# Input loads, weight splits and constants reordered at the start of an attention and mixture-of-experts layer, two vector steps moved in its ending

## The chip, the cores and the metric

The kernel runs on one core of one Trainium2 chip. The metric is the device time of one execution in microseconds. A measurement is the median of several runs; the profile comes from one further execution with its own time.

## What is computed

`x` has the shape 8 x 750 x 256, everything in fp32. Three stages follow each other for each of the 8 batch entries:

```
# 1. tokens: three shifted copies side by side, one linear layer
x = concatenate([input[:, o:o + 744, :] for o in (0, 3, 6)], axis=-1)
h = einsum('btd,od->bto', x, W) + b                       # 8 x 744 x 256
# 2. causal attention, 16 heads of 16, on the layer norm of h
h = h + softmax(mask(q k^T / sqrt(16))) v @ Wp.T + bp
# 3. four experts of width 1024, the best two of each token
logits = layernorm(h) @ wr + br
y = gelu(x @ w1[e] + b1[e]) @ w2[e] + b2[e]
c = gelu(b1) @ w2 + b2 ; c_sum = c.sum(axis=0)
out = h + sum_k gates_k * (y_sel - c_sel + c_sum)
```

`c`, `c_sum` and `b2 - c + c_sum` depend on the weights alone. The kernel calls them `crow`, `csum` and `dall`.

## The kernel before, in words

The program is written out by hand in one function, `layer`, with one block for each engine. A list of events sets the order of work, and every engine walks the same list and does its share of each event, with semaphores in between. `front_events` is the list ahead of the first batch entry, `body_events` that of one entry (it also holds the front work of the next one), and `ending` that of the experts' stage. The body runs 8 times; the last entry's rest is done in the ending, beside the first expert tiles.

**Opening.** SP (SyncE) issues twelve loads at lines 530 to 541: the token weights transposed (`tok_stage`, which lies in `prob`), the q, k and v weights, two bias rows, the token weights as they are (`tok_raw`, which lies in `spare`), the router's weights `wr_sb` (256 x 4), bias columns, the router's bias, and the output projection's weights twice (`wp_rows` in `spare`, `projw`). POOL (GpSimd) fills all constants (lines 661 to 687), among them three rows of ones in each of the four stacks `kst` (line 674), which are 3 partitions of 2976 elements. PE (TensorE) waits at the head of its block for all those constants and for five of the loads (`extra_loaded`). Then it multiplies the token weights by the router's weights, 12 products (line 1302), the projection's weights likewise, 4 products (line 1306), and the bias columns and `ones`, 6 products (line 1311). The results are extra router columns that ride along with the token product and the projection: `DA` is 256 + 4. These products are fp32, and the trace counts two records for each. DVE (VectorE) copies the results out (lines 964 to 968), and only then does ACT (ScalarE) round `tok_stage` with its new columns and `qkv_stage` into fp32r (lines 823, 824). DVE subtracts for the low halves (lines 971, 972). Every fp32 product later is made of three: high by high, high by low, low by high.

ACT loads `x` for the first entry (line 854) after both splits (`w_split` 2). POOL splits it into high and low (lines 700, 703), twice, once for each half of the 256 features. Then PE does the token product, 6 tiles of 18 matmuls (line 1329), and DVE adds the bias and takes the statistics (lines 987 to 995). POOL takes the root (line 708), DVE normalises (line 1001), PE turns the tiles (line 1349).

**q and k.** Eight `qk` events follow. For each PE multiplies, ACT, DVE and POOL cut the result into three bf16 parts (lines 902, 1015, 751, 753) in one of three buffers `parts`, and SP stores it to DRAM (line 548). `load_stack` n reads the parts back from DRAM as the stack of four heads, six DMAs for each n (line 562). It waits until the stores of its half are done. The first `mx` events (products of q and k whose row maxima DVE takes, lines 1389, 1031 and 1028) need stack 0 alone.

```
    for m in range(KC):
        for n in range(4):
            yield "qk", 4 * m + n
        yield "load_stack", 2 * m
        yield "load_stack", 2 * m + 1
```

**Ending.** `const` 0 and 1 are the products for `crow` (PE line 1462, 96 records in all; DVE line 1253). At the end of `const` 1, DVE also forms `csum` and `dall` in 8 instructions (lines 1256 to 1263). Two `flip` events turn the first tile of rows (PE 1446, ACT 950, DVE 1238), and the expert tiles start: `l1` is a first-layer product (PE 1481, gelu on ACT 935, high and low on DVE 1269 and 1271), `l2` a second-layer product (PE 1497), `y` the scaling of a finished tile on DVE (1283). `l2` number n waits for the low half of `l1` number n, and the first `l2` of a tile waits for `y` of the tile before. ACT reads `dall` at `offs` (line 945), first after `l1` 8. The last entry's projection, norm, gates, count, places, the expert table and the scatters are put beside the steps by the dictionary `BESIDE`. The table (DVE lines 1197 to 1232, 17 instructions) tells which rows the tiles from number 4 on take.

## Time and profile before

| | |
|---|---|
| median of 3 runs | 1761.87 us |
| the runs | 1755.54, 1761.87, 1763.46 us |
| the profiled execution, its own time | 1770.43 us |
| its span, from the first to the last instruction | 1768.7 us |
| busy: PE, weight loads (PEld), DVE, ACT, POOL | 86%, 67%, 62%, 40%, 47% |
| mean granted TensorE clock | 0.936 |

The profiled execution took 8.6 us more than the median. 1.7 us of its time lie outside its span. A busy share is an average over stages with different limits; the opening has hardly any PE work in it, and the ending almost nothing else. All times below are microseconds from the start of the span.

### The profile page before, as it was taken

The numbers are of one execution on the slowest core, as the hardware profiler recorded it, in microseconds if no ns is written. First come the engines' busy times: TensorE is split into PE (matmuls) and PEld (weight loads), VectorE is DVE, ScalarE is ACT, GpSimd is POOL, SyncE is SP. The second block draws the span as 40 slices with busy tenths as digits, with TensorE's granted clock in tenths as the row PEclk, the third lists the DMA queues.
The fourth block names the chain that finished last, engine by engine and source line by source line (L and its number), as shares of the span: only waits on it lengthen the run. The fifth ranks groups of instructions, "written<-read, shape, count | busy, mean of one in ns | idle before, by whom it ended". The sixth has DMA issues, their size and how long they took to land.

```text
span 1768.7 us, 33228 instructions
## 1 busy us (share of the span) xinstructions
PE 1522.5 (86%) x10648; PEld 1184.5 (67%) x10648; DVE 1100.8 (62%) x3476; ACT 707.0 (40%) x1463; POOL 837.1 (47%) x912
## 2 busy tenths in 40 slices
PE   2659898798898897898987877889999999999997
PEld 2626565474474474464654432789999999999997
DVE  1356678678678677778686571555555555555554
ACT  0104554444444544634544445133333333333332
POOL 4313434644644645736546335055455545554545
PEclk9859999898898998999998888899999999999999
DMA  2151543653643644635626675255555564645451
GB/s 89 61 136 49 153 111 102 158 134 103 154 124 106 162 118 130 162 100 163 147 78 165 151 249 177 79 177 173 201 186 186 180 204 157 215 162 188 169 189 46
DMA packets 166972, 256.24 MB, mean 145 GB/s; under 512 B 30484, under 2 KB 97998, under 8 KB 166800
## 3 DMA queue, kind: packets, MB, share of 16 engines
q1 hardware_dynamic: 108816, 166.66, 32.5%
q10 hardware_dynamic: 34368, 50.33, 9.1%
q0 software_dynamic: 23616, 37.12, 7.4%
q8 instruction: 87, 1.43, 0.3%
q14 instruction: 85, 0.70, 0.1%
HBM read 173.92 MB, written 75.29 MB: 141 GB/s over the span
## 4 chain that ended last, share of the span: by engine, by line
PE 53%; DVE 13%; DMA 11%; issue 10%; SPq 5%; ACT 4%; POOL 3%; ACTq 0%; DVEq 0%; POOLq 0%
PE yb L1497 15%; PE l1b L1481 14%; PE pab L1329 6%; PE pvb L1429 6%; PE stb L1406 4%; PE mxb L1389 4%; DMA qk_s<-parts 4%; DMA qst<-negp 4%; DVE unused L1028 4%; SPq L594 2%; DVE mxp L1031 1%; PE rb L1446 1%; SPq L562 1%; SPq L578 1%; ACT hf L935 1%
## 5 line engine op out<-in xcount | busy, mean ns | idle before, releaser
L849 ACT ACTIVATE prob<-stb 124x496 f32<-124x496 f32 (+2 forms) x832 | 397.9, 505 | 412.4 <-PE stb L1406 393.7
L1389 PE MATMUL mxb<-kst,qst 96*124 96x372 bf16 (+4 forms) x1024 | 314.6, 339 | 98.8 <-DVE mxp L1028 57.4
L1028 DVE CUSTOM_DVE_ANT_0 unused<-mxb,mask_row 124x372 bf16<-124x372 f32 (+4 forms) x768 | 351.7, 483 | 70.6 <-PE mxb L1389 67.5
L1497 PE MATMUL yb<-w2p,hp 128*128 x2448 | 334.5, 282 | 15.3 <-DVE yo L1283 15.3
L1406 PE MATMUL stb<-qst,kst 99*124 99x372 bf16 (+4 forms) x1024 | 307.3, 333 | 45.2 <-DMA qst<-negp 21.8
L1481 PE MATMUL l1b<-x2T,w1s 128*128 128x384 f32 x1632 | 338.9, 343 | 1.2 <-DVE x2T L1238 1.2
L1497 PEld LDWEIGHTS yb<-w2p,hp 128*128 128x128 f32 x2448 | 320.1, 189 | 25.9 <-issue 25.8
L935 ACT ACTIVATE hf<-l1b,b1c 128x384 f32<-128x384 f32 x272 | 158.3, 582 | 351.2 <-PE l1b L1481 347.5
L1481 PEld LDWEIGHTS l1b<-x2T,w1s 128*128 128x128 f32 x1632 | 276.6, 190 | 1.6 <-DVE x2T L1238 1.6
L1389 PEld LDWEIGHTS mxb<-kst,qst 96*124 96x124 bf16 x1024 | 138.1, 143 | 190.8 <-DVE mxp L1028 102.1
L1269 DVE CAST hp<-hf 128x384 fp32r<-128x384 f32 x272 | 107.6, 396 | 235.9 <-ACT hf L935 231.0
L1406 PEld LDWEIGHTS stb<-qst,kst 99*124 99x124 bf16 x1024 | 133.7, 140 | 172.7 <-ACT prob L849 85.6
L736 POOL TENSOR_SCALAR_AFFINE_SELECT prob<-prob 124x496 f32<-124x496 f32 x192 | 118.7, 626 | 263.0 <-ACT prob L849 261.6
L1429 PE MATMUL pvb<-prob,vaug 124*17 124x372 f32 (+2 forms) x2304 | 196.0, 458 | 3.5 <-POOL prob L736 3.5
L725 POOL DMA_INDIRECT xs<-xrow,place x96 | 132.4, 1379 | 109.8 <-issue 109.8
L1271 DVE TENSOR_TENSOR hp<-hf,hp 128x384 fp32r<-128x384 f32 x272 | 163.5, 601 | 9.4
L797 POOL DMA_INDIRECT acc<-out,xg x102 | 108.5, 1064 | 121.0 <-DMA out<-acc,xg 97.3
L1031 DVE TENSOR_REDUCE mxp<-mxb 124x1 f32<-124x372 f32 (+1 forms) x256 | 129.8, 507 | 53.2 <-PE mxb L1389 49.1
L803 POOL TENSOR_TENSOR acc<-acc,yo 128x256 f32<-128x256 f32 x102 | 82.3, 823 | 132.4 <-DVE yo L1283 71.9
L1329 PE MATMUL pab<-tokw,xp 128*124 128x260 f32 x864 | 118.5, 293 | 17.7 <-POOL xp L703 17.7
L1329 PEld LDWEIGHTS pab<-tokw,xp 128*124 128x124 f32 x864 | 110.5, 189 | 18.8 <-issue 17.7
L806 POOL DMA_INDIRECT out<-acc,xg x102 | 107.7, 1056 | 26.3 <-issue 20.7
(176 smaller groups left out, 1493.1 us busy)
## 6 DMA issues: line engine op xcount, KB each, us to landing
w1s<-ws SPq DMA_DIRECT2D x34, 2048.0 KB, 9.2
qk_s<-parts SPq DMA_DIRECT2D x64, 279.0 KB, 5.8
xg<-xs SPq DMA_DIRECT2D x34, 396.0 KB, 3.7
kst<-qk_s SPq DMA_DIRECT2D x32, 279.0 KB, 3.8
qst<-qk_s SPq DMA_DIRECT2D x32, 279.0 KB, 5.2
wraw<-in_w_all ACTq DMA_DIRECT2D x32, 256.0 KB, 6.2
ws<-whi ACTq DMA_DIRECT2D x32, 256.0 KB, 2.8
ws<-wlo ACTq DMA_DIRECT2D x32, 256.0 KB, 5.5
```

The lines of the kernel that those rows point to most:

```text
L725: pool.indirect_dma_start(out=xs, out_offset=bass.IndirectOffsetOnAxis(ap=place[:, k, i:i + 1].bitcast(u32), axis=0), in_=xrow[:, i, :], i ...
L849: act.activation(dst, src, ACT.Exp, scale=DH ** -0.5).then_inc(exp_done, 1)
L935: act.activation(hf[:, n % HFB, :], l1b[n % L1B][:, 0:TILE], ACT.Gelu, bias=b1c[:, bass.ds(owners[t] * NM + m, 1)]).then_inc(gelu_done, 1)
L1028: done = dve.tensor_tensor_reduce(out=unused[:, n % 2, e * w:(e + 1) * w], in0=src, in1=mask_row[:, T - w:T], scale=1.0, scalar=-3.0e38, o ...
L1031: done = dve.tensor_reduce(top, src, AX.X, ALU.max)
L1271: dve.tensor_tensor(hp[1][:, n % HPB, :], hf[:, n % HFB, :], hp[0][:, n % HPB, :].bitcast(fp32), ALU.subtract).then_inc(h_split, 1)
L1329: done = nc.tensor.matmul(out, lhs[x][c], rhs[w][c], start=(n == 0), stop=(n == len(steps) - 1))
L1389: done = nc.tensor.matmul(out, qst[g % NG][0:ROWS, h + e, TT * i:TT * i + TT], kst[g % NG][0:ROWS, h + e, k0:k0 + w], start=True, stop=True)
L1406: done = nc.tensor.matmul(out, kst[g][:, h, TT * j:TT * j + TT], qst[g][:, h, q0:q0 + w], start=True, stop=True)
L1429: done = nc.tensor.matmul(pvb[2 * DH * h:2 * DH * h + DH + 1, s, q0 - s * HALF:q1 - s * HALF], vaug[:, j, HG * (g % NG) + h, :], p, start= ...
L1481: done = nc.tensor.matmul(l1b[n % L1B][:, 0:TILE], w1s[t % 2][:, w, c, 128 * m:128 * m + 128], x2T[x][:, t % 2, c, :], start=(k == 0), sto ...
L1497: done = nc.tensor.matmul(yb[i][:, 0:D], hp[x][:, n % HPB, 128 * i:128 * i + 128], w2p[w][:, bass.ds(owners[t], 1), m, :], start=(m == 0 a ...
```

## The change

Five edits, all of order:

1. **Loads.** SP now issues `tok_raw` and `wr_sb` first, then `tok_stage`, bias columns, `wp_rows`, the token bias row, q, k, v, the other bias rows and `projw`. ACT issues the two loads of `x` as its first instructions. There are new semaphores: `raw_loaded` for the first two, `tokw_loaded` for `tok_stage`.
2. **Splits.** The 256 plain columns of the token weights are split without the router's columns, which are split by themselves once they are there. PE starts the 12 router products as soon as `raw_loaded` says so, and waits for the bias columns, `wp_rows` and the router's bias (`extra_loaded`, now 3 loads) only ahead of the other 10. Those 10 go to the second PSUM bank. PE's wait ahead of the token product, `w_split` 2, no longer covers the q, k and v weights.
3. **Constants.** POOL fills `ones`, splits `x`, and only then fills the other constants, the `kst` rows last. The waits for them stand where they are first used.
4. **Stack loads.** In `front_events`, `qk` 4 and 5 come ahead of `load_stack` 0 and 1.
5. **Ending.** The 8 instructions of `csum` and `dall` become an event `sum` behind step 3 of the experts, and the table moves from step 9 to step 10.

```
@@ front_events
-    yield "x_load", 0
-    for p in range(2 * KC):
-        yield "x", p
...
-    for m in range(KC):
-        for n in range(4):
-            yield "qk", 4 * m + n
-        yield "load_stack", 2 * m
-        yield "load_stack", 2 * m + 1
+    for n in range(8):
+        yield "qk", n
+        if n in (5, 7):
+            yield "load_stack", n - 5
+            yield "load_stack", n - 4
@@ ending, BESIDE
             for kind, n in BESIDE.get(at, ()):
                 yield "tail", kind, n
+            if at == 3:
+                yield "expert", "sum", 0
...
-          8: [("place", 0), ("place", 1)], 9: [("table", 0)]}
+          8: [("place", 0), ("place", 1)], 10: [("table", 0)]}
@@ gpsimd
+            pool.memset(ones[:, :], 1.0).then_inc(ones_ready, 1)
+            pool.wait_ge(ones_ready, 1)
...
+            for p in range(2 * KC):
+                emit([("x", p)], 0, 0)
+            pool.memset(vaug[:, :, :, :], 1.0).then_inc(zeroed, 1)
...
+            pool.wait_ge(route_consts, 13)
+            for g in range(NG):
+                if g:
+                    pool.wait_ge(kst_ones, g)
+                pool.memset(kst[g][ROWS:ROWS + NPART, :, :], 1.0).then_inc(kst_ones, 1)
@@ scalar
-            act.wait_ge(w_loaded, 64)
+            for c in range(KC):
+                act.dma_start(xraw[:, c, :], xT[0, 128 * c:128 * c + 128, :]).then_inc(x_loaded, 16)
+            act.wait_ge(tokw_loaded, 16)
+            act.activation(tokw[0][:, :, 0:D], tok_stage[:, :, 0:D], ACT.Copy).then_inc(w_top, 1)
             act.wait_ge(extra_evac, 1)
-            act.activation(tokw[0][:, :, :], tok_stage, ACT.Copy).then_inc(w_top, 1)
+            act.activation(tokw[0][:, :, D:DA], tok_stage[:, :, D:DA], ACT.Copy).then_inc(w_top, 1)
+            act.wait_ge(w_loaded, 48)
             act.activation(qkvw[0][:, :, :], qkv_stage, ACT.Copy).then_inc(w_top, 1)
-            act.wait_ge(w_split, 2)
+            act.wait_ge(w_split, 3)
@@ vector
+            dve.wait_ge(w_top, 1)
+            dve.tensor_tensor(tokw[1][:, :, 0:D], tok_stage[:, :, 0:D], tokw[0][:, :, 0:D].bitcast(fp32), ALU.subtract).then_inc(w_split, 1)
             dve.wait_ge(extra_full, 1)
             dve.tensor_copy(tok_stage[:, :, D:DA], pab[:, 0:24].rearrange("p (c e) -> p c e", e=NE)).then_inc(extra_evac, 1)
...
+            dve.wait_ge(w_top, 2)
+            dve.tensor_tensor(tokw[1][:, :, D:DA], tok_stage[:, :, D:DA], tokw[0][:, :, D:DA].bitcast(fp32), ALU.subtract).then_inc(w_split, 1)
+            dve.wait_ge(extra_full, 2)
+            dve.wait_ge(rows_loaded, 16 * 3)
...
@@ vector, experts
-                    if n == 1:
+                if kind == "sum":
+                    if n == 0:
                         dve.wait_ge(c_step, NE)
@@ tensor
-            pe.wait_ge(consts, 5 + NG)
-            pe.wait_ge(zeroed, 1)
-            pe.wait_ge(pvb_clear, 1)
-            pe.wait_ge(route_consts, 14)
-            pe.wait_ge(extra_loaded, 16 * 5)
+            pe.wait_ge(raw_loaded, 32)
...
+            done.then_inc(extra_full, 1)
+            pe.wait_ge(extra_loaded, 16 * 3)
+            pe.wait_ge(ones_ready, 1)
...
             pe.wait_ge(w_split, 2)
-            bank_by = [(extra_evac, 5)] + [None] * (PAB - 1)
+            bank_by = [(extra_evac, 1), (extra_evac, 5)]
```

SP's queue at the start of the program, before and then with the change (`spare` with `in_tok_W` is `tok_raw`, `prob` with `in_tok_W_T` is `tok_stage`):

```order
L530 DMA prob<-in_tok_W_T 128x6x256
L532 DMA prob<-in_Wk_T 128x2x256
L532 DMA prob<-in_Wq_T 128x2x256
L532 DMA prob<-in_Wv_T 128x2x256
L533 DMA tokb_row<-in_tok_b 124x256
L534 DMA bp_row<-in_bp 124x256
L536 DMA spare<-in_tok_W 128x2x768
L537 DMA wr_sb<-in_wr 128x2x4
L538 DMA bcol<-in_b_cols 128x2x2
L539 DMA br_row<-in_br 124x4
L540 DMA spare<-in_Wp 128x2x256
L541 DMA projw<-in_Wp_T 128x2x256
```

```order
L530 DMA spare<-in_tok_W 128x2x768
L531 DMA wr_sb<-in_wr 128x2x4
L532 DMA prob<-in_tok_W_T 128x6x256
L533 DMA bcol<-in_b_cols 128x2x2
L534 DMA spare<-in_Wp 128x2x256
L535 DMA tokb_row<-in_tok_b 124x256
L537 DMA prob<-in_Wk_T 128x2x256
L537 DMA prob<-in_Wq_T 128x2x256
L537 DMA prob<-in_Wv_T 128x2x256
L538 DMA bp_row<-in_bp 124x256
L539 DMA br_row<-in_br 124x4
L540 DMA projw<-in_Wp_T 128x2x256
```

The raw token weights moved from seventh to first place. The router's bias `br_row`, which PE waits for ahead of its last 10 products, moved from tenth to eleventh.

SP's queue at the q and k events, before and then with the change (six of the twelve loads of stacks 0 and 1 shown):

```order
L548 DMA qk_s<-parts 128x3x372 x4
L562 DMA kst<-qk_s 48x2976
L562 DMA kst<-qk_s 32x2976
L562 DMA kst<-qk_s 16x2976
L562 DMA qst<-qk_s 48x2976
L562 DMA qst<-qk_s 32x2976
L562 DMA qst<-qk_s 16x2976
```

```order
L547 DMA qk_s<-parts 128x3x372 x6
L561 DMA kst<-qk_s 48x2976
L561 DMA kst<-qk_s 32x2976
L561 DMA kst<-qk_s 16x2976
L561 DMA qst<-qk_s 48x2976
L561 DMA qst<-qk_s 32x2976
L561 DMA qst<-qk_s 16x2976
```

Two more stores stand ahead of the loads.

DVE's queue in the ending, from the last `crow` on, before; then with the change, first the same place, then the place behind step 3:

```order
L1253 TENSOR_TENSOR crow<-rb,b2row 128x256 x4
L1256 TENSOR_TENSOR csum<-crow 128x256
L1259 TENSOR_TENSOR csum<-csum,crow 128x256 x2
L1260 TENSOR_TENSOR dall<-b2row,crow 128x1024
L1263 TENSOR_TENSOR dall<-dall,csum 128x256 x4
L1238 TENSOR_TENSOR x2T<-rb,x2T 128x384 x2
L1269 CAST hp<-hf 128x384
```

```order
L1265 TENSOR_TENSOR crow<-rb,b2row 128x256 x4
L1250 TENSOR_TENSOR x2T<-rb,x2T 128x384 x2
L1282 CAST hp<-hf 128x384
L1284 TENSOR_TENSOR hp<-hf,hp 128x384
L517 TENSOR_LOAD table
```

```order
L1284 TENSOR_TENSOR hp<-hf,hp 128x384
L1089 TENSOR_SCALAR xrow<-res,mv,rstd 124x256 x3
L1269 TENSOR_TENSOR csum<-crow 128x256
L1272 TENSOR_TENSOR csum<-csum,crow 128x256 x2
L1273 TENSOR_TENSOR dall<-b2row,crow 128x1024
L1276 TENSOR_TENSOR dall<-dall,csum 128x256 x4
L1250 TENSOR_TENSOR x2T<-rb,x2T 128x384
L1282 CAST hp<-hf 128x384
```

The sums no longer stand ahead of the first tile's `x2T`; they stand ahead of the second tile's and of the high and low halves of `l1` 4. The table likewise went from ahead of the first `yo` (line 1283) to behind it and behind the halves of `l1` 10.

## Rows read from the trace of the kernel before

**Rows 1.** The page, busy time of each engine
```profile
PE 1522.5 (86%) x10648; PEld 1184.5 (67%) x10648; DVE 1100.8 (62%) x3476; ACT 707.0 (40%) x1463; POOL 837.1 (47%) x912
```
**Rows 2.** Span and mean granted TensorE clock of the core
```profile
core 0: 1768.7 us, clock 0.936
```
**Rows 3.** The chain that ended last, 0 to 110: start, us, what
```profile
11.83 2.58 POOL kst L674
...
24.45 2.49 PE pab L1311 x12
...
27.24 1.28 ACT L823
...
35.42 3.69 DMA xraw<-in_x_T
...
94.50 7.63 DMA qk_s<-parts
```
**Rows 4.** Timeline, 0 to 60: start, us, engine, line, operation, [idle before, releaser]
```profile
17.49 5.25 PE L1302 MATMUL pab<-wr_sb,spare 128*128 128x4 f32 x24 [17.49 <-POOL xrow L687]
...
28.53 1.50 ACT L823 ACTIVATE tokw<-prob 128x1560 fp32r<-128x1560 f32 x1
...
31.52 1.78 DVE L971 TENSOR_TENSOR tokw<-prob,tokw 128x1560 fp32r<-128x1560 f32 x1 [4.08 <-ACT qkvw L824]
...
44.60 15.58 PE L1329 MATMUL pab<-tokw,xp 128*124 128x260 f32 x107 [17.67 <-POOL xp L703]
```
**Rows 5.** Stretches of 1 us: length, PE clock, DMA share, GB/s
```profile
4.00:5.00 1.00, 1.00 1.10 390
...
9.00:10.00 1.00, 1.00 1.05 214
...
14.00:15.00 1.00, 1.00 0.24 83
```
**Rows 6.** Groups by form, stretches 17:27, 44.4:48.8, 53:60: count, busy, mean ns
```profile
L1302 PEld LDWEIGHTS pab<-wr_sb,spare 128*128 128x128 f32 x24 | 5.2, 331 | 17.5 <-issue 17.5
...
L1329 PE MATMUL pab<-tokw,xp 128*124 128x260 f32 x19 | 4.4, 425 | 17.7 <-POOL xp L703 17.7
...
L1329 PEld LDWEIGHTS pab<-tokw,xp 128*124 128x124 f32 x59 | 7.2, 185 | 0.0
...
L1329 PE MATMUL pab<-tokw,xp 128*124 128x260 f32 x60 | 7.4, 283 | 0.0
```
**Rows 7.** Timeline, 60 to 110
```profile
62.06 1.37 POOL L708 TENSOR_TENSOR rstd<-veps,power 124x6 f32<-124x6 f32 x1 [17.56 <-DVE veps L995]
...
96.22 0.88 PE L1389 MATMUL mxb<-kst,qst 96*124 96x372 bf16 x2 [7.47 <-DMA qst<-qk_s]
...
103.19 0.54 DVE L1031 TENSOR_REDUCE mxp<-mxb 124x1 f32<-124x372 f32 x1
```
**Rows 8.** Timeline, 1104 to 1172, the start of the experts
```profile
1120.19 0.42 DVE L1256 TENSOR_TENSOR csum<-crow 128x256 f32<-128x256 f32 x1
...
1120.80 0.49 ACT L950 ACTIVATE x2T<-rb 128x384 fp32r<-128x384 f32 x1 [15.84 <-PE rb L1446]
...
1124.12 0.55 DVE L1238 TENSOR_TENSOR x2T<-rb,x2T 128x384 fp32r<-128x384 f32 x1
...
1150.73 0.22 PE L1377 MATMUL pab<-rowsum,earlier 124*124 124x4 bf16 x1 [1.55 <-DVE rowsum L1119]
...
1158.03 0.14 DVE L1197 TENSOR_TENSOR cnt<-base,ecap 1x4 f32<-1x4 f32 x1
...
1161.56 1.25 DVE L1283 SCALAR_TENSOR_TENSOR yo<-yb,gcol,offs 128x256 f32<-128x256 f32 x3
1162.27 2.29 PE L1497 MATMUL yb<-w2p,hp 128*128 x9 [4.73 <-DVE yo L1283]
...
1166.28 1.23 PE L1497 MATMUL yb<-w2p,hp 128*128 x9
```
**Rows 9.** Stretch of 4 us in the ending: busy, then PE clock, DMA
```profile
1160.00:1164.00 4.00, 1.73 (x8) 1.73 (x9) 3.49 (x13) 0.00 (x0) 3.39 (x3) 0.50 0.34 73
```

More of the change, by code:

```diff
@@ L494, in layer @@
         extra_loaded, extra_full, extra_evac = sem("extra_loaded"), sem("extra_full"), sem("extra_evac")
+        raw_loaded, tokw_loaded, ones_ready, kst_ones = (sem(n) for n in ("raw_loaded", "tokw_loaded", "ones_ready", "kst_ones"))
         wraw_loaded, whi_ready, wlo_ready, wsplit_stored = (sem(n) for n in (
@@ L808, in expert @@
                                                 bounds_check=NB * T - 1, oob_is_err=False).then_inc(out_stored, 16)
+            for p in range(2 * KC):
+                emit([("x", p)], 0, 0)
+            pool.memset(vaug[:, :, :, :], 1.0).then_inc(zeroed, 1)
+            for m, v in ((ident, 0.0), (mask_row, 0.0), (power, -0.5)):
+                pool.memset(m[:, :], v).then_inc(consts, 1)
+            pool.wait_ge(consts, 3)
+            pool.affine_select(out=ident[:, :], in_=ident[:, :], compare_op=ALU.not_equal, fill=1.0, base=0,
+                               pattern=[[-1, 128]], channel_multiplier=1).then_inc(consts, 1)
+            pool.affine_select(out=mask_row[:, T - TT:T], in_=mask_row[:, T - TT:T], compare_op=ALU.is_ge, fill=NEG, base=0,
+                               pattern=[[-1, TT]], channel_multiplier=1).then_inc(consts, 1)
+            pool.wait_ge(consts, 5)
+            for m, v in ((earlier[:, :], 1.0), (every[:, :], 1.0), (before[:, :, :], 1.0),
+                         (restart[:, :, :], 1.0), (xrow[:, :, :], 0.0)):
+                pool.memset(m, v).then_inc(route_consts, 1)
+            for e in range(NE):
+                pool.memset(base[:, e:e + 1], float(e * CAP)).then_inc(route_consts, 1)
+            pool.wait_ge(route_consts, 9)
+            pool.affine_select(out=earlier[:, :], in_=earlier[:, :], compare_op=ALU.is_gt, fill=0.0, base=0,
+                               pattern=[[1, TT]], channel_multiplier=-1).then_inc(route_consts, 1)
+            pool.affine_select(out=before[:, :, :], in_=before[:, :, :], compare_op=ALU.is_gt, fill=0.0, base=0,
+                               pattern=[[1, NE], [-1, NE]], channel_multiplier=0).then_inc(route_consts, 1)
+            pool.memset(restart[:, :, 0:1], 0.0).then_inc(route_consts, 1)
+            pool.iota(token_id, pattern=[[TT, NT]], base=-T, channel_multiplier=1).then_inc(route_consts, 1)
+            pool.wait_ge(route_consts, 13)
[3 more added lines that the diff above has]
+                pool.memset(kst[g][ROWS:ROWS + NPART, :, :], 1.0).then_inc(kst_ones, 1)
+            pool.wait_ge(kst_ones, NG)
             over_batches(pool, emit)
@@ L1310, in _ @@
                     side = ones[:, :] if n == 2 else bcol[:, k, n:n + 1].broadcast_to([128, TT])
-                    done = nc.tensor.matmul(pab[0:TT, 40 + NE * n:40 + NE * n + NE], side, wr_sb[:, k, :],
+                    done = nc.tensor.matmul(pabs[1][0:TT, 40 + NE * n:40 + NE * n + NE], side, wr_sb[:, k, :],
                                             start=(k == 0), stop=(k == KC - 1))
@@ L1345, in emit @@
                         c, half = n % 2, n // 2
+                        if a == 0 and n == 0:
+                            pe.wait_ge(consts, 5)
                         pe.wait_ge(xn_ready, a * NT + 3 * half + 3)
@@ L1353, in emit @@
                         m, which, half = n // 4, n // 2 % 2, n % 2
+                        if a == 0 and n == 0:
+                            pe.wait_ge(w_split, 3)
                         pe.wait_ge(turn_evac, a * 4 + 2 * half + 2)
@@ L1360, in emit @@
                     if kind == "v":
+                        if b == 0 and n == 0:
+                            pe.wait_ge(zeroed, 1)
                         pe.wait_ge(turn_evac, b * 4 + 4)
@@ L1414, in emit @@
                         if o == 0:
+                            if b == 0 and g == 0:
+                                pe.wait_ge(pvb_clear, 1)
                             if g == 0:
```

67 lines of the change are left out of this document (21 added, 46 removed).

## The prediction

> **What bounds the kernel now.** I read the clock of the core first, then the page, then the chain of waits through the opening, and at last the timelines of the three places that the change touches. TensorE is busy for 1522.5 of 1768.7 us, at a mean granted clock of 0.936 [rows 1, 2], so eight batch entries and 34 expert tiles are mostly its work. The opening is different. There the chain hops from engine to engine, and nothing runs beside it. GpSimd fills constants, the last `kst` row until 14.4 and the others until 17.3. Then PE does the 44 records of router products, from 17.49 to 26.94. ACT waits for them, loads its table (1.28) and rounds (1.50), DVE subtracts (1.78, and as much again), and only at 35.0 is `x` asked for; it lands at 39.1. GpSimd splits it, and the token product starts at 44.60 [rows 3, 4]. The reader should see that five of these links do not need each other.
>
> The second place is the q and k stage. The row maxima of stack 0 could start at 96.22, when the first `mx` product runs, but DVE takes them from 103.19 on [rows 7], since it stands behind `qk` 7, which waits for the store of `qk` 4, and that store stands in SP's queue behind twelve stack loads, until 94.5, and takes 7.6 us [rows 3]. The third is the start of the experts. `x2T` waits for DVE from 1121.29, when ACT is done, to 1124.12, behind the sums; and the first `yb` product of the second tile starts 4.73 us after PE's last work, behind the table [rows 8].
>
> **Term 1, the opening: 25.0 us.** I lay the new chain out by the durations of the old one. I take the first issues at about 1 us. `x` is 768 KB and the raw token weights 786 KB, and the queues move 390 GB/s at best with the engines at a share of 1.10, that is full [rows 5]. `x` alone took 3.69 us [rows 3], of which 2.0 are its bytes at that rate and 1.7 are fixed. Both together then land at 1 + 1.7 + 4.0 = 6.7; the small router weights make it 7.7 for PE. GpSimd splits `x` in the 5.4 us between 39.1 and 44.5, so it is done near 12.1. PE's first 24 records take 5.25, until 13.0. The transposed token weights land near 9.5; with 1.28 + 1.50 on ACT and 1.78 on DVE that is 14.1, and the small copies and the split of the router columns (six steps of 0.1 to 0.2) make it 14.7.
>
> The last link is PE's other 20 records. They wait for the bias columns, `wp_rows` and the router's bias, and the latter is now the eleventh of twelve loads. Before, the loads were 3.15 MB and were still moving 83 GB/s in the 15th microsecond, so the last was in at about 14.5 [rows 5]. With 768 KB more at 390 GB/s this becomes 16.5, and the router's bias is one load of 262 KB ahead of the end, 1.2 us at the 214 GB/s of the slower stretch: 15.3. Then come 26.94 - 22.74 = 4.2 us of records [rows 3, 4], and the token product starts at 19.6 in place of 44.60. **That is 25.0 us.**
>
> The Trainium skill says it the same way (DMA: Bandwidth & Descriptors, section "Issuing engines are not separate DMA queues"): loads from the scalar and sync engines run on the same 16 DMA engines and interleave, and a second issuing engine saves only issue time. That speaks against a gain from giving `x` a queue of its own. If it were wrong, everything would land 2.0 us earlier, and the term would be 27.0.
>
> What hides the rest: the constants now follow the split, 3.1 + 2.8 us from 12.1 to 18.0, and the `kst` rows 4 x 2.6 until 28.5. GpSimd is next needed for the root, which follows the token product: 62.06 before [rows 7], 37.1 now. So 8.6 us of cover are left; without them each microsecond would count. DVE is free for the first tile once the q, k and v weights are split: copies until 20.0, then 1.75, so 21.8. The first tile leaves PE at 19.6 + 4.4 = 24.0 [rows 6]. The q, k and v splits cost nothing, since tile 0 hides them.
>
> **Term 2, stack loads behind two more stores: 4.7 us.** The time base here is the old one. Stores 4 and 5 leave at about 86.5 and 88.5, when their parts are ready, and the loads at 88.9 in place of 88.0. So stack 0 is 0.9 us later, and the two stores (571 KB) run beside its loads: 0 to 2.4 us more, by 238 GB/s in that stretch at the most. I take 0.9 + 0.8, so the first `mx` product is at 97.9 and DVE's first maximum at 98.5, in place of 103.19. Store 4 has landed by then even at 7.6 us (94.1), and `qk` 7 is through DVE. The bounds are 2.7 (full contention) and 6.0 (none, first maximum at 97.2). The next late thing is stack 0 itself.
>
> **Term 3, the ending: 4.6 us.** (a) Without the sums `x2T` starts at 1121.3 in place of 1124.12: 2.8 us. (b) The sums take from 1120.19 to 1124.2, 4.0 us, and stand now ahead of `l1` 4's halves. DVE there is busy nearly without gaps until `rowsum`, for which PE already waits 1.55 us at 1150.73 [rows 8]. Its own gaps there are 0.2 us, so this costs 3.8. (c) The table takes 1161.56 - 1158.03 = 3.5 us; behind `yo` it holds only `l1` 11's halves, which PE needs some 5 us later. Gain 3.5. (d) PE stood idle for 4.73 us there, and its granted clock in 1160 to 1164 is 0.50, the lower level of 1.2 GHz [rows 9]: nine `yb` products took 2.29, and 1.23 four microseconds later. With the idle stretch down to 1.3 us I take the clock as kept: 2.1 for the nine and the six after them. Sum 2.8 - 3.8 + 3.5 + 2.1 = 4.6. Bounds: the longer wait at `rowsum` (3.6 us) can itself bring the clock down, minus 2.1 and, if the table hides nothing, minus 3.5 more: -1. On the other side the shorter gap ahead of the first tile can keep the clock up for `l1` 0, 1 and the projection: plus 4.2, so 8.8.
>
> **Sum.** 25.0 + 4.7 + 4.6 = 34.3 us. All later work hangs on the chain, since the same events follow in the same order, so I let all of it reach the end. The profiled execution's own 1770.43 becomes 1736.1. It stood 8.6 us above the median of the runs, and the median of 1761.87 becomes 1727.6.
>
> **The rivals.**
> *The clock is up at the first token tile.* The 44 records now stand directly ahead of the token product. The first 19 matmuls took 425 ns each, later ones 283 [rows 6], so a warm start gives 2.3 us: 1725.3. Against it: 9.5 us of just such records before did not speed up. Their weight loads stayed at 331 ns, as against 185 in the fast stretch. The Trainium skill's rule (TensorE: Matmul & The Clock Gate, section "What's actually happening") is that sustained activity releases the clock. By that rule the full speed should come within this stretch; the trace so far does not bear it out for such narrow products. Chance 0.12.
> *The router's bias lands early.* If the queue does not keep its order strictly, PE's 44 records run through, from 7.7 to 17.2: 2.4 us more, 1725.2. Chance 0.10.
> *Contention and the sums eat terms 2 and 3.* Then 25.0 is left: 1736.9. For it speaks the DMA load next to stack 0 and the full DVE in the ending. Chance 0.17.
> *The clock in the body, the case on the other side.* A mean of 0.936 means that 226 of the 1768.7 us ran at the lower level. Each entry has idle stretches at its q and k stage whose length depends on how transfers fall. If the shifted start makes them longer, each further microsecond at 1.2 GHz costs up to 0.5. The gain is gone with 69 us more at the lower level, and the kernel is 0.5% (8.8 us, about what a measurement can tell) slower with 86 us more, from a mean clock of 0.912 down: 1771. Against it: the change touches nothing in the body. Chance 0.06, of which 0.04 ends within 0.5% and 0.02 beyond.
> *The change doesn't do what it says.* "Input first" would be empty if the last loads still set PE's start. They do, in part; that is in term 1 already, as the 15.3.
>
> **How the numbers follow.** Forecast 0.55, the rivals 0.12, 0.10, 0.17 and 0.06. The likeliest time is 1727.6. The largest gain by the bounds is 27.4 + 2.3 + 6.0 + 8.8 = 44.5, the smallest 23.0 (loads 2 us later) + 2.7 - 1 = 24.7. That gives 1717.4 and 1737.2. The runs shown differ by -6 and +2 from their median, so 3 us more at the lower end and 6 at the upper one, where the clock rival begins: 1714 to 1743. Faster by over 0.5%: 0.94, all cases but the clock's; within: 0.04; slower: 0.02.
>
> **What would show it.** Token product's first matmul at 19.6, within 17 to 22; `x` split done near 12; `kst` rows done before the root is asked for. From the first token matmul to the first maximum: 53.9 where it was 58.6. `x2T` directly behind ACT at the first flip; PE's wait at `rowsum` near 5 us in place of 1.55; the wait ahead of `yb` gone and its nine products at 1.2. The prediction is wrong if the token product starts after 25, if the root waits for GpSimd, or if the mean clock leaves 0.93 to 0.94 by more than 0.01.

## The result, and the profile after

The change takes 1741.53 us in the median of six runs (1728.33 to 1743.78), the kernel before 1765.38 in six (1755.54 to 1769.19), three of which are those in the table of the time before. The ratio on record is 0.9834, with a 95% interval of 0.9804 to 0.9865. That is **29.3 us less** (23.8 to 34.6), where the prediction had 34.3. It is not the ratio of the two medians, which lie only 23.9 us apart, at the lower end of that interval. Timed a second time, against eleven runs of the kernel before, the ratio was 0.9875 (0.9827 to 0.9922), or 22 us, and the medians lie 22.8 us apart. So the gain is 22 to 29 us, and no single figure of it is firmer than that.

The profiled execution is one of the six, and the fastest of them: 1728.33. Its core and the page's busy times, which answer to [rows 1, 2]:

```profile
core 0: 1726.6 us, clock 0.937
```

```profile
PE 1523.0 (88%) x10648; PEld 1185.3 (69%) x10648; DVE 1101.6 (64%) x3477; ACT 707.3 (41%) x1464; POOL 836.9 (48%) x912
```

The work is the same to within a microsecond on every engine, and the mean clock is the same. So the time went out of the gaps. The span is 42.1 us shorter, more than the median run, and the first question is which part of that belongs to the change. I cut both spans at events that every version has. From the first exponential (stack 0's softmax of entry 0) to the first constant product of the experts lies a body that no version touches.

| stretch, us | before | change | change again | front alone | front alone again |
|---|---|---|---|---|---|
| start to the first token product | 44.60 | 20.33 | 20.73 | 20.73 | 20.34 |
| from there to DVE's first maximum | 58.59 | 53.31 | 54.97 | 54.22 | 54.21 |
| to the first exponential | 25.44 | 25.47 | 25.46 | 25.46 | 25.48 |
| to the first constant product (body) | 976.87 | 960.59 | 976.38 | 980.03 | 970.06 |
| to `l1` of expert tile 4 | 107.12 | 110.67 | 110.63 | 110.47 | 110.17 |
| to the end | 556.10 | 556.23 | 555.94 | 556.65 | 556.11 |

The body took 960.6 to 980.0 us in the fourteen profiles of this study, without an edit in it, and 960.59 and 976.38 in two profiles of the very same change. The 16.3 us that it is shorter in the profile of the change are therefore chance. Nor does the new opening shorten it: the two profiles with the old opening have 976.9 and 965.8, the twelve with the new one 971.7 in the mean. What repeats is the opening, 27.5 to 29.5 us shorter up to the first exponential, and the ending, which is not shorter.

The chain that ended last, change, 0 to 78 (start, us, what). It answers to [rows 3]:

```profile
8.58 7.50 DMA br_row<-in_br
16.13 1.87 PE pab L1318 x8
17.99 2.48 PE pab L1323 x12
20.47 14.92 PE pab L1341 x108
...
67.14 5.86 DMA qst<-qk_s
73.04 0.58 PE mxb L1409
```

And the timeline of the same stretch (start, us, engine, line, operation, in brackets the idle time before and what ended it), beside [rows 4, 7]:

```profile
7.35 0.81 POOL L673 CAST xp<-xraw 128x750 fp32r<-128x750 f32 x1 [6.35 <-DMA xraw<-in_x_T]
7.46 5.28 PE L1311 MATMUL pab<-wr_sb,spare 128*128 128x4 f32 x24 [7.46 <-DMA wr_sb<-in_wr]
...
11.00 3.23 DVE L972 TENSOR_TENSOR tokw<-prob,tokw 128x1536 fp32r<-128x1536 f32 x1 [8.84 <-ACT tokw L828]
...
16.13 1.87 PE L1318 MATMUL pab<-wr_sb,spare 128*128 128x4 f32 x8 [3.39 <-DMA br_row<-in_br]
...
20.33 15.05 PE L1341 MATMUL pab<-tokw,xp 128*124 128x260 f32 x108
...
37.21 1.37 POOL L681 TENSOR_TENSOR rstd<-veps,power 124x6 f32<-124x6 f32 x1 [8.42 <-DVE veps L1007]
...
73.64 0.55 DVE L1043 TENSOR_REDUCE mxp<-mxb 124x1 f32<-124x372 f32 x1 [8.17 <-PE mxb L1409]
```

`x` is being split at 7.35, where it was still in memory at 35. PE starts its records at 7.46, then stands 3.39 us for the router's bias, which lands at 16.1. The root on GpSimd waits 8.42 us for DVE, so the constants that now stand ahead of it cost nothing. And DVE's first maximum comes 0.6 us after the first product of the maxima, directly, with 8.17 us of idle time ahead of it, where it came 7 us after [rows 7].

The start of the experts, change, beside [rows 8]:

```profile
1106.27 0.22 PE L1397 MATMUL pab<-rowsum,earlier 124*124 124x4 bf16 x1 [3.17 <-DVE rowsum L1131]
...
1106.48 2.28 PE L1521 MATMUL yb<-w2p,hp 128*128 x9
...
1115.08 1.26 DVE L1296 SCALAR_TENSOR_TENSOR yo<-yb,gcol,offs 128x256 f32<-128x256 f32 x3
...
1115.81 1.30 PE L1521 MATMUL yb<-w2p,hp 128*128 x9 [1.22 <-DVE yo L1296]
...
1158.60 0.90 PE L1470 MATMUL rb<-ident,xg 128*128 128x128 f32 x3 [3.16 <-DMA xg<-xs]
...
1159.15 2.27 PE L1505 MATMUL l1b<-x2T,w1s 128*128 128x384 f32 x6
```

The wait of 4.73 us ahead of `yb` is 1.22, and its nine products take 1.30 and no longer 2.29, all as predicted. But the wait at `rowsum` has grown from 1.55 to 3.17, and a new one of 3.16 stands 98.9 us after the first constant product, ahead of expert tile 4, for rows that are not loaded yet. After each of the two PE runs at 1.2 GHz for a few products: nine `yb` take 2.28 us in place of 1.3 behind the first wait, six `l1` take 2.27 in place of 1.3 behind the second. The granted clock says the same, in a stretch of four microseconds behind the second wait (length, busy time of PE, PEld, DVE, ACT and POOL, granted clock, DMA share, GB/s):

```profile
1160.00:1164.00 4.00, 4.00 (x17) 4.00 (x16) 1.48 (x3) 0.61 (x2) 1.41 (x3) 0.50 1.06 392
```

That is the clock that [rows 9] showed behind the old wait. It has moved, not gone.

The forecast had the wait at `rowsum` near 5 us. It is 3.17, because part of the delay shows earlier: PE also waits 1.7 us for the second tile's `x2T`, 39.7 us behind the first constant product, where the old ending has no wait of a microsecond.

### The profile page after: what moved, and what is told of

It is laid out like the page before. It is cut to its first block, busy times and chain, and to the rows that moved or that the text cites. A ratio compares the mean times of both kernels' runs of the same rounds, so it can differ in the third digit from the quotient of the medians.

```text
span 1726.6 us, 33232 instructions
## 1 busy us (share of the span) xinstructions
PE 1523.0 (88%) x10648; PEld 1185.3 (69%) x10648; DVE 1101.6 (64%) x3477; ACT 707.3 (41%) x1464; POOL 836.9 (48%) x912
## 4 chain that ended last, share of the span: by engine, by line
PE 51%; DVE 13%; issue 12%; DMA 10%; SPq 5%; POOL 4%; ACT 3%; ACTq 0%; DVEq 0%; POOLq 0%
PE yb L1521 14%; PE l1b L1505 13%; PE pab L1341 8%; PE pvb L1453 5%; PE mxb L1409 4%; PE stb L1428 4%; DVE unused L1040 4%; DMA qk_s<-parts 3%; DMA qst<-negp 3%; SPq L593 2%; POOL xs L698 2%; DVE mxp L1043 2%; SPq L561 1%; PE rb L1470 1%; ACT hf L943 1%
## 5 line engine op out<-in xcount | busy, mean ns | idle before, releaser
L1521 PE MATMUL yb<-w2p,hp 128*128 x2448 | 335.3, 282 | 12.1 <-DVE yo L1296 11.7
```

What stands on the lines that cost most here:

```text
L1521: done = nc.tensor.matmul(yb[i][:, 0:D], hp[x][:, n % HPB, 128 * i:128 * i + 128], w2p[w][:, bass.ds(owners[t], 1), m, :], start=(m == 0 a ...
```

## The experiments

**Either half alone.** The front alone is the change with the ending of before:

```diff
     yield "expert", "const", 1
+    yield "expert", "sum", 0
...
-            if at == 3:
-                yield "expert", "sum", 0
...
-          8: [("place", 0), ("place", 1)], 10: [("table", 0)]}
+          8: [("place", 0), ("place", 1)], 9: [("table", 0)]}
```

> The opening and the stack loads as in the change, the ending as before (sums behind const 1, table at step 9). My theory (the ending's two moves are worth nothing or cost: what they give to TensorE is taken back at expert tile 4, which waits for GpSimd's chain of scatters and the first tile's stores): first exponential at 99 as in the change, and from the first constant product to tile 4 about 107.1 us as before (110.7 in the change). Rival (the ending's moves gain 4.6 us as predicted and the profiles differ by chance): this stretch is 4 us longer than in the change, some 115.

Its one run took 1749.27, and its profile has the opening of the change (first exponential at 100.4) and 110.47 us from the first constant product to tile 4. That is neither the 107.1 of my theory nor the 115 of the rival. The ending alone is before with those three edits the other way round:

> The opening and the stack loads as before, sums behind step 3 and table at step 10. My theory: from the first constant product to tile 4 about 110.7 us, as in the change, so some 3.6 more than before, with a wait of TensorE for the rows of tile 4 of some 3 us. Rival (the loss in that stretch was chance): 103 to 107. First exponential at 128.6 as before.

1762.53 in one run; the opening is that of before (first exponential at 128.0), the wait for the rows of tile 4 is there (3.06), and the ending takes 110.49. So the two halves do not depend on each other, and, set beside each other, the new ending's 110.49 and 110.67 are no shorter than the old ending's 110.47.

The kernel before has 107.12 in its one profile, and the traces show where the 3.0 to 3.4 us between it and the front alone come from. Both parts are TensorE's clock. First, PE's first wait behind the constant products comes 7.9 us after the first of them, where eleven of the fourteen profiles have 9.3 to 9.5, in old and new endings alike. The first 48 of these products took 7.01 us there and 8.38 in the second profile of the front alone. Two later profiles, both with the new ending, have 8.0 and 8.1. From 2 to 4 us behind the first product the granted clock was 0.79 before and 0.50 in the front alone (length, busy time of the engines, granted clock, DMA share, GB/s; before, then front alone again):

```profile
1107.47:1109.47 2.00, 2.00 (x16) 2.00 (x15) 0.92 (x1) 0.00 (x0) 0.00 (x0) 0.79 0.14 24
```

```profile
1072.00:1074.00 2.00, 2.00 (x11) 2.00 (x11) 0.92 (x1) 0.00 (x0) 0.00 (x0) 0.50 0.13 24
```

Second, the nine `yb` products behind the wait at `rowsum` took 1.32 us before and 2.12 in the front alone, though that wait is as long in both (1.55 and 1.56):

```profile
1150.94 1.32 PE L1497 MATMUL yb<-w2p,hp 128*128 x9
```

```profile
1116.34 0.22 PE L1396 MATMUL pab<-rowsum,earlier 124*124 124x4 bf16 x1 [1.56 <-DVE rowsum L1130]
...
1116.55 2.12 PE L1520 MATMUL yb<-w2p,hp 128*128 x9
```

From the `rowsum` product to the first scatter it is 6.9 us in the four profiles whose clock stays up there, and 7.8 to 8.4 in the ten others. So in the kernel before, the one profile on which my sums rest was lucky twice in this stretch.

Eight more versions follow. The seven of them without a row in the table of medians were executed once. In the order of this text they took 1748.30, 1739.50, 1735.85, 1737.85, 1726.35, 1747.66 and 1736.42 us. A body that moves by 20 us makes such single times useless for terms of a few microseconds, so for these versions only stretches are compared.

**The old order of q and k.** The change, with `qk` and the stack loads as before:

```diff
-    for n in range(8):
-        yield "qk", n
-        if n in (5, 7):
-            yield "load_stack", n - 5
-            yield "load_stack", n - 4
+    for m in range(KC):
+        for n in range(4):
+            yield "qk", 4 * m + n
+        yield "load_stack", 2 * m
+        yield "load_stack", 2 * m + 1
```

> The change, but with load_stack 0 and 1 ahead of qk 4 and 5 again. Theory: token product at 20.3 as in the change, the first row maximum 58.6 us behind it as before (53.3 in the change), so the first exponential at 104.4 in place of 99.1. Rival (the 5.3 us came from something else in the opening, such as the earlier x of the next entry): the stretch stays at 53 to 55.

From the token product to the first maximum it takes 57.96 us, where the change and all versions with its order have 53.3 to 55.3. The timeline of this kernel has the old picture back: a product waiting in PSUM, and DVE 7.3 us late.

```profile
71.24 0.88 PE L1409 MATMUL mxb<-kst,qst 96*124 96x372 bf16 x2 [6.77 <-DMA qst<-qk_s]
...
78.58 0.53 DVE L1043 TENSOR_REDUCE mxp<-mxb 124x1 f32<-124x372 f32 x1
```

The product itself came 50.6 us behind the token product, earlier than in the versions with the new order: that is what the two stores cost stack 0. In the profile of the change it came after 52.7, in the seven others that start the token product at about the same time after 53.3 to 54.4. So the stores cost 2.1 to 3.7 us, where I had put 1.7.

**A fifth buffer for the experts' rows.** SP loads the rows of tile 4 into the buffer of tile 0, and only when the output of tile 0 is stored; four buffers are used in turn. If that is what PE waits for, one more buffer takes the wait away.

```diff
-L1B, HFB, HPB, XGB = 3, 4, 4, 4
+L1B, HFB, HPB, XGB = 3, 4, 4, 5
```

> The change with five row buffers xg in place of four, so that the rows of tile 4 no longer wait for the stores of tile 0. Theory: TensorE's wait for the rows of tile 4 (3.2 us) and the clock drop behind it (some 2.9) go, and from the first constant product to tile 4 it is about 104.7 us in place of 110.7. Rival (the wait is for the scatters themselves, or for the padding rows, not for the buffer): still about 110.

The wait at tile 4 was gone, and the stretch to tile 4 was 103.88. But the rest, tile 4 to the end, took 561.46 in place of 556.2. From 1300 to 1600 a `yb` product starts every 121.5 ns within its nine, and every 118.1 to 118.3 ns in all the others. The longer tile had moved everything that is laid out behind it in SBUF (the on-chip memory). So I put the fifth buffer by itself at the end of the layout, where it moves nothing:

```diff
-        xg = keep("xg", [128, XGB, TB, XW])
+        xg = keep("xg", [128, XGB - 1, TB, XW])
...
+        xg_more = keep("xg_more", [128, 1, TB, XW])
```

> The change with a fifth row buffer, placed behind all other buffers in SBUF, so that none of them moves (the run before had put it in the middle, and each yb matmul behind it started 121.5 ns after the last in place of 118.3). Theory (the slower yb matmuls came from the moved addresses): from the first constant product to tile 4 some 104 us, tile 4 to the end 556.2 as in the change, yb spacing 118.3 ns. Rival (the faster start itself slows the tiles, since GpSimd now trails TensorE): tile 4 to the end again near 561.

Now 104.90 to tile 4 and 556.48 behind it, spacing 118.2. PE in this kernel at tile 4, with no bracket behind it, so with no wait:

```profile
1173.11 0.49 PE L1472 MATMUL rb<-ident,xg_more 128*128 128x128 f32 x3
1173.36 1.30 PE L1507 MATMUL l1b<-x2T,w1s 128*128 128x384 f32 x6
```

The buffer is worth 5.7 us: the wait of 3.2 and some 2.5 for the products at 1.2 GHz behind it. And it shows what PE's own chain gained by the new ending when nothing else stands in its way: 104.90 against 110.17 and 110.47 with the old one. What the rows wait for can be read on GpSimd and SP, change, 1110 to 1160:

```profile
1114.66 1.79 POOL L698 DMA_INDIRECT xs<-xrow,place  x1 [20.88 <-issue]
...
1123.80 1.35 POOL L698 DMA_INDIRECT xs<-xrow,place  x1 [0.30 <-issue]
1131.82 1.35 POOL L698 DMA_INDIRECT xs<-xrow,place  x1 [6.67 <-issue]
...
1151.95 0.97 POOL L779 DMA_INDIRECT out<-acc,xg  x1 [0.30 <-issue]
```

```profile
1155.17 0.40 SPq L648 DMA_DIRECT2D xg<-xs  x1
```

Twelve scatters, of which the seventh starts 6.67 us late, then the first tile's output, then the load. From the first scatter to that load it is 40.5 us here and 41.1 before (1157.61 to 1198.76). In the change PE takes the rows 3.4 us after that load was issued, having waited for them. Before, it took them 4.8 us after it (1203.52), without a wait. So **1.3 us was all the slack** that this second chain had; read in the same way, the two profiles of the front alone have 2.4 and 0.9. From the first scatter to tile 4 it is 54.5 to 56.0 in all versions with four buffers, and 49.7 in the one with five at the end. With four buffers, then, what PE saves behind the first scatter is given back at tile 4.

**The router's bias early.** It is loaded right behind the bias columns:

```diff
             sp.dma_start(bcol[:, :, :], bcols.rearrange("(c p) k -> p c k", p=128)).then_inc(extra_loaded, 16)
+            sp.dma_start(br_row[:, :], br.partition_broadcast(TT)).then_inc(extra_loaded, 16)
...
-            sp.dma_start(br_row[:, :], br.partition_broadcast(TT)).then_inc(extra_loaded, 16)
```

> The change with the router's bias loaded fourth in place of eleventh. Theory (TensorE's last ten products of the opening wait for the last load of their three, at 16.1): they now wait for wp_rows, in at about 12 to 13, so they follow the first twelve almost directly, and the token product starts at 17.2 to 18 in place of 20.3. Rival (the load of the bias is late because the queue serves all loads at once): token product still after 19.5.

The 44 records run through, and the token product starts at 16.75, 3.6 us earlier, and earlier than I expected:

```profile
7.42 5.28 PE L1311 MATMUL pab<-wr_sb,spare 128*128 128x4 f32 x24 [7.42 <-DMA wr_sb<-in_wr]
12.56 1.85 PE L1318 MATMUL pab<-wr_sb,spare 128*128 128x4 f32 x8
...
16.75 13.48 PE L1341 MATMUL pab<-tokw,xp 128*124 128x260 f32 x98
```

**The sums on GpSimd.** In the change the sums stand on DVE behind step 3. Here the same eight operations are issued by GpSimd, right behind the first flip, with the same semaphore:

```diff
     yield "expert", "flip", (0, 1)
+    yield "expert", "sum", 0
...
-                        dve.tensor_tensor(csum[:, :], crow[:, 0, :], crow[:, 1, :], ALU.add).then_inc(c_step, 1)
+                        pool.tensor_tensor(csum[:, :], crow[:, 0, :], crow[:, 1, :], ALU.add).then_inc(c_step, 1)
```

> The change with the eight instructions of the sums on GpSimd, behind the second flip, where it is idle for some 20 us. Theory (on DVE behind step 3 they delay the gates, the places and so the scatters by about 4 us, and the longer wait at rowsum brings TensorE's clock down): the wait at rowsum falls from 3.2 to under 2 us, from the first constant product to the first scatter some 50.5 us in place of 55.0, to tile 4 some 106 in place of 110.7, with four buffers still. Rival (the scatters start late for another reason, such as the projection): scatter at 54 or later.

The operations take 7.5 us there in place of 4, and nobody waits for them. The wait at `rowsum` is back at 1.56, the first scatter comes 50.2 us after the first constant product in place of 55.0, and tile 4 after 104.65. The rows' own wait (3.10) has stayed, 4.9 us earlier.

```profile
1079.59 0.72 POOL L763 TENSOR_TENSOR csum<-crow 128x256 f32<-128x256 f32 x1 [2.96 <-DVE crow L1275]
...
1084.39 2.92 POOL L770 TENSOR_TENSOR dall<-dall,csum 128x256 f32<-128x256 f32 x4
...
1113.63 1.79 POOL L697 DMA_INDIRECT xs<-xrow,place  x1 [15.83 <-issue]
```

Not all of the 4.8 us at the first scatter is DVE's work. The `rowsum` product comes 43.3 us after the first constant product in place of 46.6, so 3.3 us are the sums. The other 1.5 are the clock: behind `rowsum` it stays up here, and in the change it falls. It would be too much to call this the effect of the shorter wait. Behind a wait of 3.16 or 3.17 the clock fell in all eight profiles that have one, but behind one of 1.52 to 1.57 it fell in two of six, both of them the front alone.

**The constants first again.** The change, with GpSimd's split of `x` behind the constants:

```diff
-            for p in range(2 * KC):
-                emit([("x", p)], 0, 0)
             pool.memset(vaug[:, :, :, :], 1.0).then_inc(zeroed, 1)
...
+            for p in range(2 * KC):
+                emit([("x", p)], 0, 0)
```

> The change with GpSimd filling all constants ahead of the split of x, as before. Theory (the order on GpSimd decides how early x is split, and 17.3 + 5.4 us is later than TensorE's last router product): split done at 22.8 and the token product at 22.9 in place of 20.3, so 2.6 us of the 24.3 come from the constants' place. DVE's subtraction of the token weights took 3.23 us in the change beside GpSimd's subtraction of x, and 1.78 before beside nothing: by the theory that the two engines hold each other up there, it takes 1.8 to 2.3 here, beside fills alone. Rival (its slower time comes from the shape of its operands, 256 columns of 260): 3.2 here too.

The token product starts at 24.18, so "constants later" is worth 3.9 us. It was later than my estimate of 22.9 because of something I had missed: DVE's subtraction for q, k and v runs beside GpSimd's last subtraction of `x`, which takes 3.17 us in place of 1.77 (timeline, this kernel):

```profile
11.01 1.76 DVE L973 TENSOR_TENSOR tokw<-prob,tokw 128x1536 fp32r<-128x1536 f32 x1 [8.85 <-ACT tokw L829]
...
20.70 1.76 DVE L986 TENSOR_TENSOR qkvw<-prob,qkvw 128x1536 fp32r<-128x1536 f32 x1
20.91 3.17 POOL L676 TENSOR_TENSOR xp<-xraw,xp 128x750 fp32r<-128x750 f32 x1
24.18 6.10 PE L1342 MATMUL pab<-tokw,xp 128*124 128x260 f32 x28 [3.93 <-issue]
```

**All three together**, with the change and the front alone beside it, six executions of each. All three is the change with the bias early, the fifth buffer at the end and the sums on GpSimd.

> The change with the router's bias loaded fourth, the sums on GpSimd and a fifth row buffer behind all others. Theory (the three act at different places and add up): token product at 16.8, first constant product to first scatter 50.2, to tile 4 some 98.9 in place of 110.7, no wait for the rows of tile 4; against the change 3.6 + 11.8 = 15 us less, so some 1726 where the change measures 1741. Rival (each was measured against a wait that another one also removes, or the experts' later tiles take it back): to tile 4 still 104 or more, under 10 us less than the change.

> The change itself once more, on the same chip as the other runs of this call. From the profiles so far: about 26 us less than before outside the body (opening 29.5, ending -3.5), so a ratio near 0.985. The body, from the first exponential to the first constant product, took between 960.6 and 980.0 in ten profiles without any edit in it: by the theory that this is chance, it lies in that range again, and not at 960.6 as in the change's first profile; the rival says that the change made the body 16 us faster.

> The opening and stack loads alone, the ending as before, once more and timed. Theory (the ending's two moves are worth nothing): its ratio to before is within 0.002 of that of the change in this call. Rival (the moves cost or gain 4 us and more): apart by 0.0025 or more.

| kernel | median of 6, us | ratio to before (95%) | start to first exponential | first constant product to tile 4 |
|---|---|---|---|---|
| before (11 runs) | 1768.66 | | 128.63 | 107.12 |
| front alone | 1742.40 | 0.9861 (0.9817 to 0.9905) | 100.03 | 110.17 |
| change | 1745.89 | 0.9875 (0.9827 to 0.9922) | 101.16 | 110.63 |
| all three | 1729.14 | 0.9781 (0.9742 to 0.9819) | 96.93 | 99.78 |

The change and the front alone cannot be told apart (ratios 0.0014 apart, within the 0.002 expected): the whole gain is the front's. The body of the change took 976.38 us this time, so that rival is out. All three is 16.8 us faster than the change beside it. The stretches give 4.2 for the opening and 10.9 for the ending, 15.1 together. In the ending of all three both waits are dealt with, at `rowsum` (back to 1.57) and at the rows of tile 4 (none):

```profile
1110.91 0.22 PE L1398 MATMUL pab<-rowsum,earlier 124*124 124x4 bf16 x1 [1.57 <-DVE rowsum L1143]
...
1162.97 0.49 PE L1471 MATMUL rb<-ident,xg_more 128*128 128x128 f32 x3
```

**The table alone.** The change, with the sums back behind the second constant product; only the table stays a step later.

> The change with the sums back at const 1 and the table alone moved. Theory (what the table's move gives TensorE, 3.5 us and the clock, is taken back at tile 4, which waits for GpSimd): no wait of 4.7 us ahead of the second tile's first yb product, but one of 3 to 6 for the rows of tile 4, and from the first scatter to tile 4 again 55 to 56 us. Rival (the table's move is a gain by itself and the loss was the sums'): from scatter to tile 4 under 53.

The `x2T` wait of 4.06 is back, `rowsum` has 1.52, `yb` 1.23, the first scatter comes after 53.1 and tile 4 after 108.08. The wait for the rows is there as well:

```profile
1167.67 0.55 PE L1469 MATMUL rb<-ident,xg 128*128 128x128 f32 x3 [3.06 <-DMA xg<-xs]
```

From the first scatter to tile 4 it is 55.0, as the theory said, and the rival's 53 is out.

The scatter comes 1.6 us earlier than in the front alone (54.7), but the table's move did not do that. In the old order DVE starts the table only after the first scatter has started (before: the table from 1158.03 on [rows 8], the scatter at 1157.61), so it cannot hold it up. The `rowsum` product comes after 46.3 us in both kernels. What differs is the clock behind it:

```profile
1116.51 0.22 PE L1396 MATMUL pab<-rowsum,earlier 124*124 124x4 bf16 x1 [1.52 <-DVE rowsum L1130]
...
1116.72 1.32 PE L1520 MATMUL yb<-w2p,hp 128*128 x9
```

The nine products take 1.32 here and 2.12 in the front alone. With the clock up the scatter follows `rowsum` by 6.9 us, as it did before the change with the table in its old place; with the clock down by 8.4. The flip's move brings PE's first `l1` product 3.1 us forward (19.6 in place of 22.7 behind the first constant product), and the sums on DVE behind step 3 take 3.3 of it back at `rowsum`.

## Why the prediction was right, and where it was not

**The forecast** was 1727.6 with 1714 to 1743, faster. The first timing's median of 1741.53 lies inside, near the upper end, and the second's of 1745.89 just above it. In gain it was 34.3 against 29.3 by the first ratio, 23.9 by its medians, and 22 to 23 the second time. That the time fell inside the range owes something to its width: the sum was too high by all of term 3. The rival without terms 2 and 3 (25.0 us) is nearer to the measured gain than my own case, for a reason of which it had only half: term 2 came, term 3 did not.

**Term 1, 25.0 predicted, 24.3 measured (23.9 in two of the others).** The chain of the opening came out as laid out: `x` split done at 12.6 for 12.1, 24 records by 12.7 for 13.0, the bias at 16.1 for 15.3, the token product at 20.33 for 19.6. The 0.7 us missing are the bias load, which sets PE's last records as forecast (15.3 and 4.2 make 19.5, not the 19.6 of the text); the run with the bias early shows that this wait was worth 3.6, more than the 2.4 I gave it. DVE's split took 3.23 us for my 1.78 and cost nothing, because PE was later still. The bytes moved at up to 420 GB/s for my 390. The rule that a second issuing engine adds no bandwidth (the Trainium skill, DMA: Bandwidth & Descriptors, section "Issuing engines are not separate DMA queues") agrees with the row: `x` was in at 7.35, 0.65 after my 6.7. By my estimate a queue that added bandwidth would have brought it 2.0 us ahead of that.

**Term 2, 4.7 predicted, 5.3 measured in the first profile, 3.6 in the second**, and 3.0 to 4.7 between the run with the old order and the eight with the new one that start the token product within 0.5 us of it. The mechanism is the one named: without `qk` 7's wait in DVE's way, the next late thing is stack 0. The two stores cost its loads 2.1 to 3.7 us for my 1.7. My bounds of 2.7 and 6.0 do not follow from their own steps, which give 3.1 and 5.5 (stack 0 later by 0.9 and by 0 to 2.4, the first maximum 0.6 behind the product). Some of the 5.3 is the clock: the records of the token product fall from 0.42 to 0.28 us each 4.1 us behind its start in the change, and 5.6 us behind it before.

**Term 3, 4.6 predicted, nothing measured**: 110.2 and 110.5 with the old ending, 110.5 to 110.9 with the new; and where the constant products were through early, 107.1 with the old one (before) and 108.6 with the new (bias early). Its parts were nearly right. (a) The flip gained 3.1 for my 2.8. (b) The sums cost 3.3 at `rowsum` for my 3.8, so `rowsum` comes after 46.6 us, where the front alone has 46.3 and 46.5. (c, d) PE's wait went from 4.73 to 1.22 and the clock stayed up, the 5.6 of PE's time that I counted; but the first scatter comes after 54.9, as in the front alone (54.7 and 54.9). The step that failed is the sentence behind the sum: "All later work hangs on the chain, since the same events follow in the same order, so I let all of it reach the end." In the ending two chains run side by side, PE's, and GpSimd's from the first scatter over the first output to the load of tile 4's rows. The second did not get shorter or start earlier, and before it had 1.3 us of slack, so that no wait showed there; the place where the two meet again, 40 us on, lay beyond the stretch that I read. On PE's own chain the term is right: with the fifth buffer, which takes the second chain away, the new ending is 5.3 to 5.6 shorter than the old one, for my 4.6. Without it the gain is given back at tile 4: a little over half as a wait of 3.2, the rest as products at 1.2 GHz.

**A base of one profile.** 107.12 before against 110.2 to 110.5 of the same ending in two later profiles made my bookkeeping look 3.5 us worse than it was, and the body made it look 16 better. The first is the size of a term, the second three times one. Of the first, 1.4 us are the first 48 constant products and about 1.5 the clock behind `rowsum`. The bound that I gave for term 3, in which a longer wait at `rowsum` brings the clock down, came true in the change; but the front alone has the same fall behind a wait that did not grow.

**The rivals.** The clock was not up at the first token tile: it lasts 4.4 us (20.33 to 24.7), as before, directly behind 44 narrow records. The bias did not land early. Neither contention nor the sums ate the terms, as that rival had it: term 2 is there, and term 3 was lost at tile 4. The mean clock was 0.929 to 0.937 in the six runs, inside the bound that I had set for it.

**What stays open.** Why the seventh scatter starts some 7 us late was not tried, though it stands in the chain that bounds the ending with four buffers. Nor is it known why the clock rose sooner under the constant products in three profiles of fourteen, nor why it fell behind the short wait at `rowsum` in the front alone and not in the four others. The fifth buffer at the end, the bias early and the sums on GpSimd have one profile each by themselves and one together.

## What to carry to other kernels

Before a gain in one engine's waits is let through to the end, look for the next place where that engine meets another chain (a buffer that comes round, a load that waits for an output), and measure that chain from its own start: if it is as long as before, the gain ends there. Moving work from before a wait to after it gives nothing where the engine has no gap there: on DVE the sums took back what the flip had gained, on idle GpSimd they cost nothing. Before a difference of a microsecond or two is put down to an edit, look at the granted clock on both sides of it. And compare stretches, cut at events that all versions have, in two or three profiles of each: here an untouched body moved by 20 us from profile to profile.

## What the runs showed of the hardware

**Two-input operations of DVE and GpSimd hold each other up.** DVE's subtraction of 128x1536 took 1.76 us beside GpSimd's fills and 3.23 beside GpSimd's subtraction of 128x750; the latter took 1.77 in the change and 3.17 beside a DVE subtraction in the run with the constants first. Each time the one that came second took about its own time and what was left of the other's: 1.6 us were left for DVE, which took 1.5 longer, and 1.55 for GpSimd, which took 1.4 longer. The Trainium skill has the rule (SBUF — State Buffer, section "Who interferes with whom"): a DVE instruction with two SBUF inputs contends with a GpSimd instruction that reads SBUF, not with one that only writes it. The rows agree, also in that the fills, which read nothing, cost DVE nothing.

**Where a tile lies changes how fast matmuls follow each other.** With the rows' tile grown from four buffers to five in the middle of the layout, nine `yb` products were 121.5 ns apart and not 118.2, 5.3 us over 30 tiles. With the same buffer at the end it did not happen (two profiles). Which tile's new place does it was not tried.

**The same wait does not always bring the clock down.** Behind waits of 1.52 to 1.57 us at `rowsum` the nine `yb` products took 2.12 us in the second profile of the front alone and 1.32 both before and with the table alone. The dearer case moved the first scatter by 1.5 us with no edit near it.

**The clock record says 1.00 ahead of its first change**, though the matmuls of the first token tile last 4.4 us, their length at the lower level in [rows 6]. At the start of a program the length of a known matmul is the better witness.
